# A four-layer graph network: layers 1 and 2 written out, layer 2 reordered by chunks, its sum taken over high and low halves

## What is computed

```python
hi = jnp.einsum('bsh,hk->bsk', x, W1[:H])
hj = jnp.einsum('bsh,hk->bsk', x, W1[H:])
h = jax.nn.relu(hi[:, :, None, :] + hj[:, None, :, :] + b1)
y = jnp.einsum('bijk,kl->bijl', h, W2) + b2
y = _layernorm(y, gamma, beta)
out = jnp.einsum('bij,bijh->bih', adj, y)
# and around it: x = _layernorm(x + out)
```

## Time and profile before

| what | us |
|---|---|
| median of 3 runs | 1713.37 (1710.48 to 1713.9) |
| the profiled execution | 1708.26 |
| its span | 1706.5 |
| layer 1, first gather to last sum | about 182 to 1041 |
| layer 2, first load to last squares | about 1052 to 1581 |
| busy over the span: PE, DVE, ACT | 1460.6 (86%), 1196.0 (70%), 959.0 (56%) |

### The profile page before, as it was taken

How to read it: one execution, slowest core, us unless ns; L and a number is a source line. 1 busy time by engine, 2 the same in 40 slices (tenths; PEclk the granted TensorE clock), 3 DMA queues, 4 the chain that set the end, 5 groups by cost and what they waited for, 6 DMA issues and landing times. The chain is left out here.

```text
span 1706.5 us, 32127 instructions
## 1 busy us (share of the span) xinstructions
PE 1460.6 (86%) x9657; PEld 1247.2 (73%) x9721; DVE 1196.0 (70%) x2322; ACT 959.0 (56%) x2535; POOL 5.4 (0%) x24
## 2 busy tenths in 40 slices
PE   3664788989899898998989975999999999998564
PEld 3553556868787677877868774899999999997554
DVE  4886677677777777677777644566666666666788
ACT  2564786656556565565655312566666666665554
POOL 0000000000000000000000000000000000000000
PEclk9997899999999999999999997999999999999877
DMA  2220567868668676776767655867667667671122
GB/s 69 75 62 14 214 253 283 302 237 289 246 259 300 225 275 244 275 295 227 276 245 277 253 183 195 315 236 254 252 235 256 247 238 255 245 248 46 56 75 68
DMA packets 137523, 366.82 MB, mean 215 GB/s; under 512 B 12896, under 2 KB 71904, under 8 KB 137440
## 3 DMA queue, kind: packets, MB, share of 16 engines
q1 hardware_dynamic: 137040, 365.81, 59.7%
q10 hardware_dynamic: 400, 0.00, 0.0%
HBM read 231.54 MB, written 134.22 MB: 214 GB/s over the span
## 5 line engine op out<-in xcount | busy, mean ns | idle before, releaser
L863 DVE TENSOR_TENSOR b_wt<-bank,b_aT 128x512 f32<-128x512 f32 (+1 forms) x192 | 109.5, 599 | 142.3 <-PE bank L703 140.2
L1153 DVE TENSOR_REDUCE c_var<-c_ysq 128x4 f32<-128x512 f32 (+1 forms) x192 | 114.1, 594 | 117.0 <-ACT c_ysq L1101 95.7
L661 PE MATMUL wide<-b_vv,put_w 128*128 128x512 f32 (+1 forms) x384 | 171.8, 529 | 24.5 <-DVE b_vv L838 22.6
L1043 PE MATMUL wide<-W2c,c_h 128*128 128x128 f32 x1280 | 174.4, 275 | 4.5 <-issue 0.2
L838 DVE TENSOR_TENSOR b_vv<-bank,b_vv 128x512 f32<-128x512 f32 (+1 forms) x192 | 114.3, 599 | 86.9 <-ACT b_vv L759 83.7
L1043 PEld LDWEIGHTS wide<-W2c,c_h 128*128 128x128 f32 x1280 | 170.0, 193 | 4.3
L687 PE MATMUL bank<-b_wt,b_SITl 128*128 128x136 f32 x1280 | 162.8, 283 | 7.4 <-DVE b_wt L863 7.4
L687 PEld LDWEIGHTS bank<-b_wt,b_SITl 128*128 128x128 f32 x1280 | 158.7, 192 | 14.0 <-DVE b_wt L863 9.4
L703 PE MATMUL bank<-b_grl,b_SJl 128*128 128x128 f32 x1280 | 154.6, 276 | 5.1 <-ACT b_os L786 3.4
L1073 PEld LDWEIGHTS bank<-c_z,c_SIT 128*128 128x128 f32 x1280 | 153.9, 193 | 5.5 <-DVE c_z L1161 2.3
L1073 PE MATMUL bank<-c_z,c_SIT 128*128 128x128 f32 x1280 | 154.5, 276 | 2.1 <-DVE c_z L1161 2.1
(11 more groups left out here) (213 smaller groups left out, 2949.8 us busy)
## 6 DMA issues: line engine op xcount, KB each, us to landing
si_d<-b_SI SPq DMA_DIRECT2D x64, 640.0 KB, 3.0
sj_d<-b_SJ SPq DMA_DIRECT2D x64, 640.0 KB, 4.0
sit_d<-b_SIT SPq DMA_DIRECT2D x64, 640.0 KB, 5.0
b_SJl<-sj_d SPq DMA_DIRECT2D x64, 640.0 KB, 5.3
b_SITl<-sit_d SPq DMA_DIRECT2D x64, 640.0 KB, 5.7
c_SJ<-sj_d SPq DMA_DIRECT2D x64, 640.0 KB, 4.0
c_SI<-si_d SPq DMA_DIRECT2D x64, 640.0 KB, 5.2
c_SIT<-sit_d SPq DMA_DIRECT2D x64, 640.0 KB, 4.2
```

The lines of the kernel that those rows point to most:

```text
L661: pe.matmul(out, e.put_w[:, pos, :], vv[:, (pos + k) % 2, 0:width(k)], start=(pos == 0), stop=False)
L863: v.tensor_tensor(wt[:, mb, 4 * k:4 * k + rr, 0:P].rearrange("p r (h f) -> p r h f", h=HEADS), ring[k][:, 0:P * rr].rearrange("p (r h f) - ...
L1043: d = pe.matmul(bY[k][:, a:a + P], h[:, k, a:a + P], e.W2c[:, :], start=False, stop=(j == last))
L1153: v.tensor_reduce(var[:, k, 0:r], ysq[:, k, 0:width(k)].rearrange("p (j f) -> p j f", f=P), AX.X, ALU.add).then_inc(sum_ok, 1)
```

## The change

`every_step` loses its loop: all steps are written out, in layers 1 and 2, and every semaphore target is a constant. Layer 1 is otherwise unchanged. In layer 2:

- The sum is taken in one pass. ACT copies z chunk by chunk into the first 128 columns of `zz` in F32R (`keep_high`), DVE writes z less that into the other 128 (`keep_low`). SIT is declared F32R. Ten F32R products of 256 columns replace the ten float32 ones of 128 columns. The result has a high and a low part of 128 columns for each of the four graphs of a batch, so it takes two PSUM banks (`duo`). Once a batch ACT copies the low parts out (`rest`) and DVE adds them to the high parts, ahead of gamma.
- The sum runs two graphs behind (m = n - 2), the projection two ahead; `hi` and `lo` have four slots.
- The gather has two banks in turn instead of three (`pair_bank`). A step's order on PE: transpose (n+2), gather 1, sum (n-2), MLP 0, projection (n+2), gather 2, MLP 1, gather 0 of n+1, MLP 2. ACT and DVE finish chunk 2 and the second half of chunk 1 of a graph in the next step.

```diff
@@ -324,16 +324,10 @@
     return range(4 * k, min(4 * k + 4, TILES))
 
 
...
+def every_step(eng, step, extra, early=1):
+
+
+    for n in range(-early, B + extra):
         step(n // 8, n % 8, False)
@@ layer1_packed, and the same for its tensor, scalar and vector queues @@
-                every_step(sp, step, 13, 2)
+                every_step(sp, step, 13)
@@ -936,11 +930,11 @@
         s = Packed()
         s.SI = sb("SI", [P, 4, ECAP], F32R)
         s.SJ = sb("SJ", [P, 4, ECAP], F32R)
...
+        s.SIT = sb("SIT", [P, 4, TILES, P], F32R)
         s.xin = sb("xin", [P, 2, P])
         xT = sb("xT", [P, P])
...
+        hi = sb("hi", [P, 4, 2 * P], F32R)
+        lo = sb("lo", [P, 4, 2 * P], F32R)
         s.junk = sb("junk", [P, P])
         s.mean = sb("mean", [P, Q])
         s.res = sb("res", [P, Q, P])
@@ -948,6 +942,8 @@
         ysq = sb("ysq", [P, CHUNKS, CHUNK])
         var = sb("var", [P, CHUNKS, 4])
         z = sb("z", [P, 2, TILES, P])
+        zz = sb("zz", [P, 2, TILES, 2 * P], F32R)
+        rest = sb("rest", [P, Q, P])
         bb = sb("bb", [P, Q, P])
         sj_in = [sem(f"sj_in{b}") for b in range(4)]
         si_in = [sem(f"si_in{b}") for b in range(4)]
@@ -968,18 +964,24 @@
         root_ok = sem("root_ok")
         inv_ok = sem("inv_ok")
         z_ok = sem("z_ok")
+        zh_ok = sem("zh_ok")
+        zl_ok = sem("zl_ok")
+        rest_ok = sem("rest_ok")
         o_mm = sem("o_mm")
         o_read = sem("o_read")
         seq_c = sem("seq_c")
...
+        bU = e.banks[0:2]
+        bP = e.banks[2]
         bY = e.banks[5:8]
+        bO = e.duo[:, :].rearrange("p (q a f) -> p q a f", q=Q, f=P)
 
         def gathered(n, inner):
             return inner or 0 <= n < B
 
         def summed(n, inner):
+            return inner or 2 <= n <= B + 1
+
+        def followed(n, inner):
             return inner or 1 <= n <= B
 
         def part(n, pos, inner, k):
@@ -988,6 +990,9 @@
 
         def batches(K, pos):
             return 8 // Q * K + pos // Q
+
+        def pair_bank(pos, k):
+            return bU[(pos + k) % 2]
 
         def rounds(K, pos):
@@ -1007,10 +1012,10 @@
                     if inner or 0 <= m < B:
                         if inner or m >= 4:
                             sp.wait_ge(o_mm, m - 3)
...
+                        sp.dma_start(s.SIT[:, (pos - 1) % 4, :, :].bitcast(F32),
                                      e.sit_v[:, m, :].rearrange("p (j i) -> p j i", i=P)).then_inc(sit_in[(pos - 1) % 4], 16)
 
...
+                every_step(sp, step, 1, 2)
 
             @block.gpsimd
             def _(pool):
@@ -1022,15 +1027,17 @@
                     n = 8 * K + pos
                     g = n + 1
                     A, N, S = gathered(n, inner), gathered(n + 1, inner), summed(n, inner)
...
+                    N2 = gathered(n + 2, inner)
+
+                    def gather(n, pos, k):
+                        w, cs, r = width(k), chunk(k), pos % 4
+                        bank = pair_bank(pos, k)
+                        if inner or 3 * n + k >= 2:
+                            pe.wait_ge(h_ok, 3 * n + k - 1)
+                        pe.matmul(bank[:, 0:w], hi[:, r, 0:P], s.SJ[:, r, cs], start=True, stop=False)
+                        pe.matmul(bank[:, 0:w], lo[:, r, 0:P], s.SJ[:, r, cs], start=False, stop=False)
+                        pe.matmul(bank[:, 0:w], hi[:, r, P:2 * P], s.SI[:, r, cs], start=False, stop=False)
+                        pe.matmul(bank[:, 0:w], lo[:, r, P:2 * P], s.SI[:, r, cs], start=False, stop=True).then_inc(s.u_mm, 1)
 
                     def mlp(k):
                         pe.wait_ge(h_ok, 3 * n + k + 1)
@@ -1043,40 +1050,40 @@
                             d = pe.matmul(bY[k][:, a:a + P], h[:, k, a:a + P], e.W2c[:, :], start=False, stop=(j == last))
                         d.then_inc(y_mm, 1)
 
...
+                    if N2:
+                        pe.wait_ge(s.x_ok, n + 3)
+                        if inner or n >= -1:
+                            pe.wait_ge(lo_ok, n + 2)
+                        pe.transpose(bP[:, 0:P], s.xin[:, pos % 2, :], e.ident[:, :]).then_inc(s.xT_mm, 1)
+                    if A:
+                        gather(n, pos, 1)
+                    if S:
+                        m, r = n - 2, (pos - 2) % 4
+                        pe.wait_ge(zl_ok, 3 * n - 3)
+                        pe.wait_ge(sit_in[r], 16 * (2 * K + (pos - 2) // 4 + 1))
+                        if r == 0 and (inner or m >= Q):
+                            pe.wait_ge(o_read, batches(K, pos))
+                        for j in range(TILES):
+                            d = pe.matmul(bO[:, r, :, :], s.SIT[:, r, j, :], zz[:, pos % 2, j, :],
+                                          start=(j == 0), stop=(j == TILES - 1))
+                        d.then_inc(o_mm, 1)
                     if A:
                         mlp(0)
...
+                    if N2:
+                        pe.wait_ge(xT_ok, n + 3)
+                        pe.matmul(bP[:, P:3 * P], xT[:, :], e.W1s[:, :, :], start=True, stop=True).then_inc(p_mm, 1)
+                    if A:
+                        gather(n, pos, 2)
                         mlp(1)
                     if N:
...
+                        pe.wait_ge(lo_ok, g + 1)
+                        pe.wait_ge(sj_in[(pos + 1) % 4], rounds(K, pos + 1))
+                        pe.wait_ge(si_in[(pos + 1) % 4], rounds(K, pos + 1))
+                        gather(g, pos + 1, 0)
                     if A:
                         mlp(2)
 
...
+                every_step(pe, step, 7, 2)
 
             @block.scalar
             def _(act):
@@ -1086,56 +1093,77 @@
                     n = 8 * K + pos
                     g = n + 1
                     A, N, N2 = gathered(n, inner), gathered(n + 1, inner), gathered(n + 2, inner)
...
+                    N3 = gathered(n + 3, inner)
+
+                    def rectify(n, pos, k):
                         act.wait_ge(s.u_mm, 3 * n + k + 1)
                         if inner or n >= 1:
                             act.wait_ge(y_mm, 3 * n + k - 2)
...
+                        act.activation(h[:, k, 0:width(k)], pair_bank(pos, k)[:, 0:width(k)], ACT.Relu,
                                        bias=e.b1c[:, 0:1]).then_inc(h_ok, 1)
 
...
+                    def square(n, k):
                         act.wait_ge(y_mm, 3 * n + k + 1)
                         if inner or n >= 1:
                             act.wait_ge(sum_ok, 3 * n + k - 2)
                         act.activation(ysq[:, k, 0:width(k)], bY[k][:, 0:width(k)], ACT.Square).then_inc(ysq_ok, 1)
 
...
+                    def root(n, k):
                         sd = var[:, k, 0:len(tiles(k))]
                         act.wait_ge(sum_ok, 3 * n + k + 1)
                         act.activation(sd, sd, ACT.Sqrt, bias=e.eps[:, 0:1], scale=1.0 / P).then_inc(root_ok, 1)
 
...
+                    def keep_high(n, b, k):
+                        act.wait_ge(z_ok, 3 * n + k + 1)
+                        if inner or n >= 2:
+                            act.wait_ge(o_mm, n - 1)
+                        act.copy(zz[:, b, tiles(k).start:tiles(k).stop, 0:P],
+                                 z[:, b, tiles(k).start:tiles(k).stop, :]).then_inc(zh_ok, 1)
+
+                    F = followed(n, inner)
+                    if F:
+                        square(n - 1, 2)
+                    if N2:
+                        act.wait_ge(s.xT_mm, n + 3)
                         act.copy(xT[:, :], bP[:, 0:P]).then_inc(xT_ok, 1)
...
+                    if F:
+                        keep_high(n - 1, (pos - 1) % 2, 1)
+                    if A:
+                        rectify(n, pos, 1)
+                    if F:
+                        root(n - 1, 2)
+                    if A:
+                        square(n, 0)
+                    if N2:
+                        act.wait_ge(p_mm, n + 3)
+                        if inner or n >= 2:
+                            act.wait_ge(s.u_mm, 3 * n - 3)
+                        act.copy(hi[:, (pos + 2) % 4, :], bP[:, P:3 * P]).then_inc(hi_ok, 1)
+                    if F:
+                        keep_high(n - 1, (pos - 1) % 2, 2)
+                    if A:
+                        rectify(n, pos, 2)
+                        root(n, 0)
+                    if part(n, pos, inner, 1):
+                        act.wait_ge(o_mm, n - 1)
+                        if inner or n > Q + 1:
+                            act.wait_ge(o_read, batches(K, pos) - 1)
+                        act.copy(rest[:, :, :], bO[:, :, 1, :]).then_inc(rest_ok, 1)
                     if part(n, pos, inner, 5):
                         squares(act, e, s, batches(K, pos) - 2, range(0, Q // 2))
                     if part(n, pos, inner, 6):
                         squares(act, e, s, batches(K, pos) - 2, range(Q // 2, Q))
...
+                    if N3:
+                        normalise_x(act, e, s, K, pos + 3, inner or n >= -1)
+                    if A:
```

(73 more changed lines are left out.)

102 lines of the change are left out of this document (8 added, 94 removed).

## The result

| | us |
|---|---|
| median after, 4 runs | 1684.47 (1678.95 to 1686.86) |
| median before, 4 runs beside them | 1713.15 (1710.48 to 1713.9) |
| ratio after / before | 0.9836, 95% interval 0.9821 to 0.9851 |
| the profiled execution after, its span | 1684.72, 1683.0 |

The account below looks back on a forecast made before the run. PE bound layer 2 before; after, the ACT-DVE chain of handovers would. 18.9 (steps) + 1.5 and 3.3 (loops) - 0.5 (end) = 23.2 us off 1713.4 gave 1690 us; own range 1680 to 1700, 8 in 10 1660 to 1714.

Parts of the forecast that it names:

- The steady step: Layer 2: one graph's step takes 6.96, 7.83, 8.35, 7.37 us by position, mean 7.63 instead of 7.93, saving 18.9 us.
- The saving on PE: Layer 2's sum: ten one-pass products take 1.17 us instead of 2.23, saving PE 1.06 us a graph.
- PE's other needs: Layer 2: chunk 0's h, lows for the sum and the projection two ahead were claimed to be met earlier.
- A: Rival for layer 2: PE stays the bound at 6.87 us a graph, 1642 us; chance 0.13 including the way to it.
- the ring: Layer 2: ACT's copies and DVE's subtractions and scales wait on each other in turn, setting a mean step of 7.63 us.
- B: Rival for layer 2: DVE instructions stand full durations apart, mean step 8.18, 1725 us; chance 0.17 including the way to it.
- C: Rival for layer 2's sum: 0.22 us a product, PE needs 7.93 us a graph as before, 1709 us; chance 0.08.
- First gather to last MLP: Layer 2's main stretch: 18.9 us saved over 63 steps and 1.5 us from its loop.
- The ends: Layer 2: first loads cost 0; work in series behind the last MLP adds about 0.5 us, bounds -1 and +2.
- Layer 1's loops: Layer 1: writing out saves 0.081 us on each of 40 looped steps, 3.3 us.
- the last step of the sum: Whole kernel: the before median's 5.1 us above its profiled execution was carried over, 1713.4 - 23.2 = 1690 us.

Follow-up runs that it names:

- e3: The kernel after, same order and written out, but the sum again ten float32 products without copies and subtractions; 1701.27 us, ratio to before 0.9940.
- e4: The kernel after without DVE's three subtractions a graph, low halves being zeros written once; 1639.05 us, ratio to before 0.9573.
- e10: e7 with ACT's scaling of x moved earlier in the step; 1655.51 us, ratio to before 0.9678.
- e7: The kernel after with ACT's high-half copies moved behind rectify and root, DVE's subtractions behind the scale; 1656.48 us, ratio to before 0.9674.
- e5: The kernel after with one unused ACT copy of 512 elements a step ahead of the chunk 1 high-half copy; 1683.76 us, ratio to before 0.9834.
- e6: The kernel after with one unused ACT copy of 512 elements a step behind the chunk 1 high-half copy; 1705.0 us, ratio to before 0.9955.
- e1: The kernel before with layers 1 and 2 written out, nothing else changed; 1704.03 us, ratio to before 0.9954.
- e2: The kernel after with the hardware loops put back in layers 1 and 2; 1694.56 us, ratio to before 0.9897.
- e8: e7 with two of a batch's products moved from DVE to POOL; 1646.76 us, ratio to before 0.9628.
- e9: e8 with ACT's scaling of x moved earlier in the step; 1646.94 us, ratio to before 0.9629.

## Why the prediction was right, and where not

**The steady step.** Forecast by position 6.96, 7.83, 8.35, 7.37, mean 7.63; measured at the copy 6.94, 7.79, 8.35, 7.37, mean 7.61. That is closer than the 0.15 us a step that I had allowed. The terms held one by one: copy of 512 at 0.62 (forecast 0.61), of 256 at 0.41 (0.40), subtraction 0.68 to 0.69 (0.69), the ten products 1.2 us (1.17). By the Trainium skill (VectorE: DVE Perf Modes, The TRN2 errata) a copy of 512 would be 0.61 us, an estimate; the trace agrees with its 0.62. The saving on PE shows in the experiments too: e3 and e4 keep PE full at 7.92 and at 6.87 to 6.93, about 1.0 us apart, where I had 1.06.

Two of the signs that I named did not show. I expected the pattern 7.0, 7.8, 8.3, 7.4 at the transposes; it stands at ACT's copy, and the transposes have 7.33 to 7.75. And I expected PE to be idle 0.76 us a graph, mostly ahead of the MLP of chunk 1; it is idle 0.55, and nearly half of that stands at the transpose, behind ACT's scaling of x. I had looked at PE's other needs and left that one out. No run moves it in this order; in e10, where it was moved, the mean step did not change.

**Mechanism.** e4 to e7 show it: without the subtractions PE is the bound at 6.9 (e4); work in the wait is free and work behind the copy costs 0.30 a step (e5, e6); the same work in another order gives 0.44 a step (e7). A bound by the sum of DVE's or ACT's work would not have moved in e7, and would have been the same in e5 and e6.

**The rivals.** *A* (PE the bound, 6.87) is what e4 does, not the change; it showed only in five of the first nine steps, 6.87 to 6.88 each, before the batch work begins and while the ring, at 6.5 to 6.9, is still shorter than PE. *B* (full durations, 8.18) is ruled out: the three rows of DVE start 0.60 apart at durations of 0.68. The Trainium skill's rule in VectorE: DVE Perf Modes, The DRAIN you can't avoid, read without the exception that it makes for an operation that is not held, would have given B's time; the trace has 0.60 where the next instruction's wait is already met. *C* (0.22 a product, 7.93) is ruled out by 1.2 us for ten.

**First gather to last MLP.** Forecast -18.9 - 1.5 = -20.4, measured -28.05. By the experiments (first gather to last MLP: before 510.5, e1 508.9, e3 503.1, after 482.5) the loops are 1.6 and the one-pass sum 20.6, close to the forecast; the order's 5.8 I had at 0. I had multiplied one steady step by 63 and left out that the first steps of the new order are short (one starts 3.06 us behind the other, and 5.93, 6.38 and 5.70 follow, where before had 8.98, 7.73, 8.01) and that one more sum lies behind the last MLP, where it is paid again.

**The ends.** Forecast +0.5, measured +5.1: 1.4 ahead of the first gather, 3.6 behind the last MLP. The 1.4 is how long the first loads took (the gather waits for a DMA; 6.3 us in e3, 6.4 in e1, which have nothing else there), so I put it down to scatter: over all kernels this stretch is 6.0 to 8.4 us. The last graph's sum starts 5.5 us behind the last MLP (1540.93 to 1546.46), since root, scale, copy and subtraction of its chunks stand in series; before, it was 2.1. In the timeline after:

```profile
1539.68 0.40 PE L1047 MATMUL wide<-b2x,ones 128*128 128x256 bf16 x1 [0.81 <-ACT c_h L1102]
1539.87 1.06 PE L1050 MATMUL wide<-W2c,c_h 128*128 128x128 f32 x4
...
1546.46 2.50 PE L1067 MATMUL duo<-c_zz,c_SIT 128*128 128x256 f32 x10 [3.40 <-DVE c_zz L1198]
...
1549.01 0.59 ACT L1151 COPY c_rest<-duo 128x512 f32<-128x512 f32 x1 [3.05 <-PE duo L1067]
...
1558.87 1.49 SPq L1654 DMA_DIRECT2D d_ain<-in_adj_dram  x3
```

In the timeline before, the last sum waited 2.12 us:

```profile
1570.39 3.64 PE L1073 MATMUL bank<-c_z,c_SIT 128*128 128x128 f32 x20 [2.12 <-DVE c_z L1161]
...
1582.59 1.49 SPq L1611 DMA_DIRECT2D d_ain<-in_adj_dram  x3
```

Both last sums meet a fallen clock, which the forecast did not have: the granted clock is 0.50 from 1546.5 us on in after, and from 1571.5 on in before, where the sum has run for 1.1 us. The ten products take 2.50 us there, by duration, where they took 1.36 inside the layer, and the twenty passes 3.64 where they took 2.39, so the one-pass sum saves 1.1 us here too.

So a gain of 7.65 and a loss of 4.6 that the forecast did not have partly cancel: layer 2's -23.0 against a forecast of -19.9 is 3.1 us off in sum only.

**Layer 1's loops.** Forecast 3.3 us. The 40 looped steps took 527.06 before, 529.2 in e2, and written out either 522.8 to 522.9 (after, e3, e8, e9, e10) or 524.6 (e1, e4, e5, e6, e7). The written-out kernels differ among themselves because a few steps of this layer have two values: 15.8 us at a granted clock of 0.89 or 14.25 at 1.00, and 16.9 at 0.90 or 15.3 at 1.00. Within these 40 steps e2 has no such short step, before and the second group have one, the first group two. Compared with as many short steps, the loops cost 2.4 us (before against e1) to 3.0 (e2 against the others, 1.6 us put back for each short step). So the 3.3 was the right size, a little high.

The whole layer differs by more, 878.1 before against 872.3 to 873.0 in e3, e8, e9 and e10: 5.1 to 5.8 us. At least 1.6 of it is the clock: all ten written-out profiles have two short steps in the layer, the two looped ones one and none. Whether writing out brings them is open.

The profiled pair shows only -1.0 there because of one step. The 12th interval of layer 1 on PE, before and after:

```profile
269.81:283.88 14.07, 10.50 (x68) 7.88 (x67) 9.73 (x15) 9.66 (x17) 0.00 (x0) 1.00 1.00 366
```

```profile
270.30:287.24 16.94, 13.36 (x69) 10.26 (x68) 9.84 (x15) 9.67 (x17) 0.00 (x0) 0.80 1.00 357
```

The same work takes 14.07 us at a granted clock of 1.00 and 16.94 at a mean of 0.80. With that fall in both, e2 (looped) has 883.7 us in the layer and the written-out kernels 877.1 to 878.4, 5.3 to 6.6 us; about 3 of that is again their two short steps.

**The whole.** The profiled pair gained 23.5 us against 23.2 forecast, and that is luck in part: layer 2 gave 3.1 more than forecast, layer 1 gave 2.3 less, because of the fall of the clock (2.9). The medians gained 28.7. What was off there is the last step of the sum, where I carried the before kernel's distance between its median and its profiled execution (5.1 us) over to the kernel after, whose median stands 0.25 us below its profiled execution. With one profile of each, the runs don't show what sets these distances.

## What to carry to other kernels

Where three engines pass work round in fixed queues, the busy shares of before only bound the answer; walking one step by start-to-start distances gave the mean to 0.02 us. Walk the first and the last steps as well, because every link added to the ring is paid in series when it drains. And ask what is queued behind each new instruction: the same instructions one place later took off another 1.6% (e7), and a filler in either place tells where there is room. Before two profiles are set against each other, look whether the clock of each step is the same in both.

## What the runs showed of the hardware

- **A clock fall at the same step, in some executions only.** The 12th interval of layer 1 takes 14.06 to 14.07 us at clock 1.00 in the profiles of before, e3, e8, e9 and e10, and 16.8 to 16.9 at a mean of 0.80 in those of after, e1, e2, e4, e5, e6 and e7. In after the clock stands at half for 6.8 us from 280.1; PE had waited 0.97 us before its product at 274.66 and 1.50 before the one at 277.92. Before has the same two waits, 0.96 and 1.50, and no fall. The DMA engines are full in both. Other steps of that layer have two values as well: 14.25 (1.00) or 15.8 (0.89), 15.3 (1.00) or 16.9 (0.90). Layer 1's work is the same in e7 and e10. What decides between the two values stays open; no run tried to set it.
- **POOL beside DVE.** Where POOL's products of 512 (1.04 and 1.49 us) ran beside DVE's subtraction, it took 937 ns instead of 682 (e8, 13 of 108; e9 the same). The scale that also ran beside POOL in that time kept its 0.69 us.
- **Loops cost more in the order of after.** In layer 2 they cost 5.1 us there (e2 to after), in the old order 2.5 (before to e1).
